# Routed experts: lists in tile order, and the gather of tile t+6 asked for ahead of the scatter-add of tile t

## The chip, the core and the metric

The kernel is one program on one core of a Trainium2 chip. The metric is its time on the device in microseconds (us). One core has five engines that run their own instruction streams and meet in semaphores: PE (TensorE, matmuls; its weight loads are listed as PEld), DVE (VectorE), ACT (ScalarE), POOL (GpSimd) and SP (SyncE, which here only issues transfers). Transfers are carried out by 16 DMA engines. In the profile "q" behind an engine's name is its sequencer.

## What is computed

Sixteen sequences of 56 tokens (896 tokens, width 512) attend to 1500 context rows each; then every token goes through a mixture of 16 experts, of which it takes 4, and through a shared expert.

```python
def _L0_xattn_ref(text, features, Wq, bq, Wk, bk):
    Q = jnp.einsum('btx,dx->btd', text, Wq) + bq
    K = jnp.einsum('bpx,dx->bpd', features, Wk) + bk
    scores = jnp.einsum('btd,bpd->btp', Q, K) * scale
    return jnp.einsum('btp,bpd->btd', jax.nn.softmax(scores, axis=-1), features)

def _L0_ffn_ref(hidden_states, gate_w, bias, Wg, Wu, Wd, Sg, Su, Sd):
    scores = jax.nn.sigmoid(x @ gate_w.T) + bias
    topk_w, topk_idx = jax.lax.top_k(scores, TOPK)
    topk_w = topk_w / (jnp.sum(topk_w, axis=-1, keepdims=True) + 1e-20)
    cw = jnp.sum(jax.nn.one_hot(topk_idx, E, dtype=x.dtype) * topk_w[..., None], axis=1)
    z = jax.nn.silu(jnp.einsum('th,eih->eti', x, Wg)) * jnp.einsum('th,eih->eti', x, Wu)
    out = jnp.einsum('eti,ehi->th', z * cw.T[:, :, None], Wd)
    return out + jax.nn.silu(x @ Sg.T) * (x @ Su.T) @ Sd.T

x = x + _L0_xattn_ref(_layernorm(x), ctx_4096, Wq, bq, Wk, bk)
x = x + _L0_ffn_ref(_layernorm(x), gate_w, bias, Wg, Wu, Wd, Sg, Su, Sd)
```

## The kernel before

**Stages.** Until about 262 us the program does attention, pair of sequences by pair. Then come seven tiles of 128 tokens through the shared expert (tiles 0 to 6), and from about 320 us the routed tiles: tile numbers 7 to 40, 34 tiles in all. A routed tile is up to 128 tokens of one expert; an expert has one or more tiles in a row. Which tokens a tile holds is known only once all tokens are gated, so the kernel builds lists (`list_rows`) and a plan of small tables (`lay_tables`, read into registers by `entry`).

**One routed tile.** POOL gathers the tile's 128 rows from `h_rows` in DRAM into `taken[i]` (`gather`, L444; i is the parity, so there are two buffers). PE transposes it into bank b4 (`taken_transpose`, four matmuls of L500). ACT rounds it to `taken_hi` (L908), DVE makes the rest `taken_lo` (L1299). PE multiplies with the expert's weights into b6 or b7 (`up_hi`, `up_lo`, L680), ACT and DVE make `z_rows`, PE transposes that (L703), ACT and DVE split it again into `zt_hi` (L918) and `zt_lo` (L1315), and PE does the second product (`down`, L680) into one of two banks. ACT copies the result to `y_sb` (`keep_y`, L926, two buffers), and POOL adds it to the output rows in DRAM (`add`, L459, a scatter-add by an indirect DMA).

**The software pipeline.** PE's step goes: transposition of z of tile t-1, `up_lo(t)`, transposition of tile t+1, `down(t-1)`, `up_hi(t+1)`. ACT's step goes: `z_to_hi(t-1)`, `half(t)`, `taken_to_hi(t+1)`, `keep_y(t-2)`, `name_add(t-2)`, `more_thirds(t+1)`. DVE's: `z_to_lo(t-1)`, `silu_rows(t)`, `taken_to_lo(t+1)`, `take_weight(t+1)`, `name_take(t+3)`, `more_thirds(t+1)`. `more_thirds` splits the next expert's weights into a rounded part (ACT, L897, `w_hi`) and the rest (DVE, L1280, `w_lo`), a third of an expert at a time; SP loads them (L383, `w_raw`, three buffers). `keep_y(t)` waits for `added[i]`, that is until the scatter-add of tile t-2 has landed. `down(t)` waits for `keep_y(t-2)`.

**What sets the order on POOL.** The queue is written out by hand: four adds of the shared expert, two gathers, and so on, then a loop of `add(t)`, `gather(t+5)`. `add(t)` waits for the adds of all earlier experts to land (table `T_FIRST`), for its row numbers `add_at` (ACT, `name_add`, L931) and for `y_sb`. `gather(t)` waits for its row numbers `take_at` (DVE, `name_take`, L1306), and DVE writes these only after it has read tile t-2's weights.

## Time and profile before

| | us |
|---|---|
| median of 3 runs | 547.0 (546.81 to 549.09) |
| the profiled execution, its own time | 546.24 |
| its span, from the first to the last instruction | 544.5 |
| PE busy | 481.4 (88%) |
| POOL busy | 119.3 (22%) |
| DVE, ACT busy | 260.0, 155.8 |

The span is the time in which instructions ran; 1.74 us of the execution's own time lie around it. A busy PE is the lower bound that everything else has to hide under. In the views below, a timeline row reads: start in us, length in us, engine, line, operation, what is written <- what is read, and in brackets how long the engine had been idle and what ended that.

### The profile page before, as it was taken

How to read it: one execution, taken by the hardware profiler on the slowest of the kernel's cores; microseconds unless marked ns; L12 is line 12 of the kernel's file. 1: busy time of each engine (PE TensorE's matmuls, PEld its weight loads, DVE VectorE, ACT ScalarE, POOL GpSimd, SP SyncE). 2: the span in 40 equal slices, each digit the busy share in tenths (PEclk: the TensorE clock that was granted, in tenths of full speed). 3: DMA queues.
4: the chain of work that ended last, by engine and by line, in shares of the span. 5: the costliest groups of instructions: out<-in, count | busy, mean ns of one | idle time of the engine just before them, and what ended most of it. 6: DMA issues, size and time to landing. Idle time of an engine off the chain costs nothing.

```text
span 544.5 us, 10804 instructions
## 1 busy us (share of the span) xinstructions
PE 481.4 (88%) x2472; PEld 291.5 (54%) x2473; DVE 260.0 (48%) x707; ACT 155.8 (29%) x303; POOL 119.3 (22%) x100
## 2 busy tenths in 40 slices
PE   4999999999999999998789869779998898899960
PEld 1565354453636363543358636567776666676740
DVE  3223345462737354352537864625565466555420
ACT  0001321020202020210213253435455456444430
POOL 1000000000000000000002233335554465335531
PEclk9989999999999999999899979979999899899985
DMA  9999999999999999999646676785858687445452
GB/s 212 393 419 427 398 424 415 409 427 396 424 402 426 403 422 404 422 426 415 258 127 174 150 202 191 235 254 94 221 100 265 137 207 210 78 88 98 98 64 32
DMA packets 28231, 149.04 MB, mean 274 GB/s; under 512 B 4072, under 2 KB 4200, under 8 KB 16424
## 3 DMA queue, kind: packets, MB, share of 16 engines
q1 hardware_dynamic: 15832, 123.08, 57.1%
q0 software_dynamic: 8720, 20.21, 20.5%
q10 hardware_dynamic: 3664, 5.57, 3.3%
q8 instruction: 7, 0.11, 0.1%
q14 instruction: 8, 0.07, 0.0%
HBM read 133.84 MB, written 15.01 MB: 273 GB/s over the span
## 4 chain that ended last, share of the span: by engine, by line
PE 49%; DMA 33%; issue 7%; DVE 3%; ACT 2%; POOLq 1%; ACTq 1%; POOL 1%; DVEq 1%; SPq 0%
DMA ctx_cols<-in_ctx_t 15%; PE b L680 13%; PE scores L550 11%; PE b L574 8%; DMA taken<-h_rows,take_at 8%; DMA out<-y_sb,add_at 5%; PE b L538 4%; PE b L500 4%; PE scores L512 2%; PE scores L680 2%; PE b L564 1%; DMA w_qk<-in_wk 1%; DMA out<-y_sb,shared_at 1%; DMA h_rows<-h 1%; POOL out L459 1%
## 5 line engine op out<-in xcount | busy, mean ns | idle before, releaser
L550 PE MATMUL scores<-ctx_cols,g_t 128*64 128x500 f32 x384 | 85.2, 586 | 2.6 <-DMA ctx_cols<-in_ctx_t 2.5
L574 PE MATMUL b<-ctx_rows,probs_t 125*64 125x512 f32 (+1 forms) x384 | 86.0, 598 | 0.0
L459 POOL DMA_INDIRECT out<-y_sb,add_at x34 | 54.5, 1604 | 89.0 <-ACT add_at L931 46.8
L423 POOL TENSOR_TENSOR rstd<-var_eps,neg_half 128x1 f32<-128x1 f32 x16 | 8.8, 549 | 268.4 <-DVE var_eps L1022 268.4
L680 PE MATMUL b<-w_hi,taken_hi 128*128 x136 | 56.2, 414 | 1.1 <-ACT taken_hi L908 1.1
L680 PE MATMUL b<-w_lo,taken_hi 128*128 x136 | 54.8, 403 | 0.0
L1280 DVE TENSOR_TENSOR w_lo<-w_raw,w_hi (+1 forms) x33 | 39.7, 1223 | 30.2 <-ACT w_hi L897 26.6
L550 PEld LDWEIGHTS scores<-ctx_cols,g_t 128*64 128x64 f32 x384 | 26.1, 136 | 51.8 <-issue 46.0
L574 PEld LDWEIGHTS b<-ctx_rows,probs_t 125*64 125x64 f32 (+1 forms) x384 | 26.3, 137 | 48.0 <-issue 47.1
L444 POOL DMA_INDIRECT taken<-h_rows,take_at x34 | 42.7, 1257 | 28.4 <-DVE take_at L1306 20.2
L897 ACT CAST w_hi<-w_raw (+1 forms) x33 | 33.8, 1047 | 29.0 <-PE b L680 9.1
L500 PE MATMUL b<-cst,taken 128*128 128x128 f32 x164 | 26.6, 287 | 17.1 <-DMA taken<-h_rows,take_at 15.2
L680 PE MATMUL b<-w_hi,taken_lo 128*128 x136 | 40.0, 416 | 0.0
L1053 DVE TENSOR_REDUCE row_max<-scores 128x1 f32<-128x1500 f32 x8 | 13.8, 1721 | 50.4 <-PE scores L550 50.4
L836 ACT COPY h_t_now<-b 128x512 f32<-128x512 f32 x7 | 4.1, 585 | 110.6 <-PE b L500 110.6
L500 PEld LDWEIGHTS b<-cst,taken 128*128 128x128 f32 x164 | 19.5, 146 | 28.3 <-issue 25.8
L1299 DVE TENSOR_TENSOR taken_lo<-b,taken_hi 128x512 fp32r<-128x512 f32 x41 | 28.1, 685 | 11.6 <-ACT taken_hi L908 11.6
L538 PE MATMUL b<-xn_t,w_fold 128*128 128x128 f32 x256 | 32.0, 286 | 1.4 <-ACT xn_t L820 1.4
L680 PEld LDWEIGHTS b<-w_hi,taken_hi 128*128 128x128 f32 x136 | 26.8, 197 | 11.0 <-issue 4.9
L908 ACT CAST taken_hi<-b 128x512 fp32r<-128x512 f32 x41 | 24.0, 587 | 30.1 <-PE b L500 28.6
L538 PEld LDWEIGHTS b<-xn_t,w_fold 128*128 128x128 f32 x256 | 30.7, 200 | 1.9 <-issue 1.0
L918 ACT CAST zt_hi<-b 128x256 fp32r<-128x256 f32 x41 | 15.2, 371 | 54.4 <-PE b L703 54.1
(213 smaller groups left out, 677.2 us busy)
## 6 DMA issues: line engine op xcount, KB each, us to landing
ctx_rows<-in_ctx SPq DMA_DIRECT2D x48, 1024.0 KB, 19.5
ctx_cols<-in_ctx_t SPq DMA_DIRECT2D x32, 1500.0 KB, 22.8
w_raw<-in_experts SPq DMA_DIRECT2D x11, 1536.0 KB, 7.5
h_rows<-h ACTq DMA_DIRECT2D x16, 115.5 KB
taken<-h_rows SPq DMA_DIRECT2D x7, 264.0 KB, 3.1
out<-xs ACTq DMA_DIRECT2D x2, 784.0 KB
shared_raw<-in_shared SPq DMA_DIRECT2D x1, 1536.0 KB, 32.4
xs<-in_x ACTq DMA_DIRECT2D x12, 112.0 KB
```

The source lines that it names most:

```text
L444: nc.gpsimd.indirect_dma_start(taken[i][:, :], None, h_rows[:, :], bass.IndirectOffsetOnAxis(ap=take_at[i][:, 0:1], axis=0)).then_inc(gath ...
L459: nc.gpsimd.indirect_dma_start(out[:, :], bass.IndirectOffsetOnAxis(ap=add_at[i][:, 0:1], axis=0), y_sb[:, i * DIM:(i + 1) * DIM], None, c ...
L500: last = nc.tensor.transpose(bank[:, k * P:(k + 1) * P], src[:, k * P:(k + 1) * P], ident)
L538: last = nc.tensor.matmul(b7[:, m * P:(m + 1) * P], w_fold[:, k, m * P:(m + 1) * P], xn_t[:, k, :], start=(k == 0), stop=(k == KD - 1))
L550: last = nc.tensor.matmul(scores[HALF * b:HALF * (b + 1), n, 0:CHUNK], g_t[:, k, HALF * b:HALF * (b + 1)], ctx_cols[:, at:at + CHUNK], sta ...
L574: last = nc.tensor.matmul(b3[HALF * b:HALF * (b + 1), :], probs_t[0:rows_in(p), at:at + HALF], ctx_rows[0:rows_in(p), g, b, c * DIM:(c + 1 ...
L680: return nc.tensor.matmul(bank, a[:, k, :], w[:, bass.ds(at + k * n, n)], start=start, stop=stop)
L897: nc.scalar.copy(w_hi[:, bass.ds(at, THIRD)], w_raw[:, bass.ds(at, THIRD)]).then_inc(hi_ready, 1)
L908: nc.scalar.copy(taken_hi[:].rearrange("p k n -> p (k n)"), b4[:, :]).then_inc(taken_hi_ready, 1)
L918: nc.scalar.copy(zt_hi_cols[:], b5[:, 0:INNER]).then_inc(zt_hi_ready, 1)
L1280: nc.vector.tensor_tensor(w_lo[:, bass.ds(at, THIRD)], w_raw[:, bass.ds(at, THIRD)], w_hi[:, bass.ds(at, THIRD)], ALU.subtract).then_inc(l ...
L1299: nc.vector.tensor_tensor(taken_lo[:].rearrange("p k n -> p (k n)"), b4[:, :], taken_hi[:].rearrange("p k n -> p (k n)"), ALU.subtract).th ...
```

## The change

- **Lists in tile order.** The row numbers of all lists (`place_at`) are transposed by PE (`lay_places`), copied by ACT (`keep_places`), and multiplied by a 0/1 matrix `tile_picks` (`pick_tiles`), so that `tile_at` and `tile_to` hold one column per tile. `name_take` and the naming of the add then read a column by the tile number. The tables `T_COL` and `T_EXPERT` and the reads of them into registers are gone; `take_weight` picks the expert's column by a comparison (one DVE instruction on 128x16). Two matmuls are added to `lay_tables`, two small DVE instructions (`keep_picks`) behind the copy of the plan.
- **POOL.** The loop is `gather(t+6)`, then `add(t)`. A gather also waits for `tt_ready`, that is until PE has transposed tile t-2, which freed its buffer. `add_at` is now copied by POOL itself, in `add`, after the own parity's earlier add has landed; `add` then waits for that copy. ACT's `name_add` is gone. In the opening, gathers 7 and 8 stand before `add_shared(3)`, and `gather(12)` stands before the loop.
- **DVE.** `take_weight` and `name_take` stand before `silu_rows` in the step.
- **SP.** The first two weight loads are issued back to back, on two semaphores; the second no longer waits for the first to land.

On POOL, in the loop over routed tiles, one half of the loop body before (out is the kernel's output, y_sb a tile's result, added0 and added1 count landed adds):

```order
L323 TENSOR_LOAD plan
L323 ISA x2
L451 ISA
L453 ISA [waits added0]
L455 REGISTER_ALU [waits added1]
L457 REGISTER_ALU [waits add_named]
L459 DMA out_0<-y_sb,add_at1 1024x512 [waits ysb_ready]
L442 REGISTER_ALU
L444 DMA taken0<-h_rows,take_at0 128x528 [waits take_named]
```

and the same half now:

```order
L463 REGISTER_ALU [waits take_named]
L465 DMA taken1<-h_rows,take_at1 128x528 [waits tt_ready]
L331 ISA
L331 TENSOR_LOAD plan
L331 ISA x2
L472 ISA
L474 ISA [waits added1]
L474 COPY add_at1<-tile_to 128x1
L476 ISA
L478 REGISTER_ALU [waits added0]
L482 DMA out_0<-y_sb,add_at1 1024x512 [waits ysb_ready,add_named]
```

The gather moved ahead of the add and got a wait on PE's transposes; the copy of `add_at` moved from ACT to POOL.

On ACT, from the copy of a result to the next third of weights, before:

```order
L926 COPY y_sb<-b3 128x512 [waits added0]
L323 ISA
L323 TENSOR_LOAD plan
L323 ISA x2
L931 ISA
L931 COPY add_at0<-list_to 128x1
L323 ISA
L323 TENSOR_LOAD plan
L323 ISA x2
L939 COMPARE_AND_BRANCH
L942 ISA [waits yt_ready]
```

and now:

```order
L968 COPY y_sb<-b3 128x512 [waits added0]
L331 ISA
L331 TENSOR_LOAD plan
L331 ISA x2
L981 COMPARE_AND_BRANCH
L984 ISA [waits yt_ready]
```

One table read and the copy of `add_at` left the step; the wait for the landed add stayed in front of the copy of the result.

The diff, cut to its core:

```diff
...
                 sp.dma_start(w_raw[:, bass.ds(at, WFREE)],
-                             experts[bass.ds(e, 1), :, :].rearrange("a p n -> (a p) n")).then_inc(raw_loaded, 16)
-                sp.wait_ge(raw_loaded, (k + 1) * 16)
+                             experts[bass.ds(e, 1), :, :].rearrange("a p n -> (a p) n")
+                             ).then_inc(raw_first if isinstance(k, int) and k == 0 else raw_loaded, 16)
+
+            def raw_there(k):
+                sp.wait_ge(raw_loaded, k * 16)
                 sp.sem_inc(raw_ready, THIRDS)
...
             load_raw(1)
+            sp.wait_ge(raw_first, 16)
+            sp.sem_inc(raw_ready, THIRDS)
+            raw_there(1)
             sp.wait_ge(yt_ready, SHARED)
             load_raw(2)
+            raw_there(2)
             n_turns = sp.value_load(plan[0:1, T_TURNS:T_TURNS + 1], min_val=TOPK, max_val=EXPERTS)
                 load_raw(k)
+                raw_there(k)
...
+                pool.wait_ge(added[t % 2], t // 2 * 16 + 16)
                 pool.wait_ge(ysb_ready, t + 1)
...
                 settle(pool)
+                pool.wait_ge(tt_ready, t - 1)
+                settle(pool)
                 nc.gpsimd.indirect_dma_start(
...
                 first = entry(pool, T_FIRST, t - SHARED, TILES + SHARED)
-                pool.wait_ge(added[0], pool.snap((first + 1) // 2 * 16 + 16, min_val=16, max_val=16 * TILES))
+                pool.wait_ge(added[i], t // 2 * 16 + 16)
                 settle(pool)
-                pool.wait_ge(added[1], pool.snap(first // 2 * 16 + 16, min_val=16, max_val=16 * TILES))
-                settle(pool)
-                pool.wait_ge(add_named, t - (SHARED - 2))
+                nc.gpsimd.tensor_copy(add_at[i][:], tile_to[:, bass.ds(t - SHARED, 1)]).then_inc(add_named, 1)
+                others = first // 2 if i == 0 else (first + 1) // 2
+                pool.wait_ge(added[1 - i], pool.snap(others * 16 + 16, min_val=16, max_val=16 * TILES))
                 settle(pool)
                 pool.wait_ge(ysb_ready, t + 1)
+                settle(pool)
+                pool.wait_ge(add_named, t + 1)
                 settle(pool)
...
             add_shared(2)
-            add_shared(3)
             pool.wait_ge(init_stored, 16)
             pool.wait_ge(h_stored, PAIRS * 32 + 16)
-            pool.wait_ge(plan_ready, 1)
-            n_inner = inner_pairs(pool)
             gather(SHARED, 1)
             gather(SHARED + 1, 0)
+            add_shared(3)
             add_shared(4)
             add_shared(6)
+            gather(SHARED + 5, 0)
+            pool.wait_ge(tiles_named, 1)
+            pool.wait_ge(plan_ready, 1)
+            n_inner = inner_pairs(pool)
             with pool.Fori(0, n_inner - 1) as pair:
                     t = pair * 2 + (SHARED + k)
+                    gather(t + 6, 1 - k)
                     add(t, 1 - k)
-                    gather(t + 5, k)
             t = n_inner * 2 + (SHARED - 2)
-            add(t, 1)
-            gather(t + 5, 0)
-            for k in range(1, 6):
+            for k in range(6):
                 add(t + k, 1 - k % 2)
...
                 last.then_inc(table_rows_ready, 1)
+                for at, column in ((C_PICK, place_col), (C_EXPERT, expert_t)):
+                    last = nc.tensor.matmul(scores[:, 0, at:at + AHEAD], column[:].to_broadcast([P, P]),
+                                            ident[:, 0:AHEAD], start=True, stop=True)
+                last.then_inc(picks_ready, 1)
+
+            def lay_places():
+
+                pe.wait_ge(plan_ready, 1)
+                pe.wait_ge(places_ready, 1)
+                nc.tensor.transpose(scores[:, 2, 0:P], place_at[:], ident).then_inc(places_laid, 1)
+
+            def pick_tiles():
+
+                pe.wait_ge(places_kept, 1)
+                nc.tensor.matmul(scores[:, 2, P:P + AHEAD], place_t[:], tile_picks[:], start=True, stop=True
+                                 ).then_inc(tiles_picked, 1)
...
             shared_transpose(6)
+            lay_places()
             down(4, 0, shared_hi, shared_lo, 0)
+            pick_tiles()
             up_hi(6, 0, shared_hi, shared_lo, 0)
...
             taken_to_hi(6)
+            keep_places()
             keep_y(3, 1)
...
                 keep_y(t - 2, i)
-                if not isinstance(t, int):
-                    name_add(t - 2, i)
                 more_thirds(t + 1)
-            act.wait_ge(list_named, 1)
             more_thirds(SHARED)
...
                 ch.link(nc.vector.scalar_tensor_tensor(raw_at[:], lists[:, :, 0], float(P), lists[:, :, 1], ALU.mult, ALU.add))
-                ch.mark(nc.vector.tensor_tensor(list_at[:, 0:LISTS], raw_at[:], fill[:], ALU.add))
-                ch.link(nc.vector.tensor_tensor(place_at[:], raw_at[:], fill[:], ALU.add))
-                ch.link(nc.vector.tensor_scalar(wrapped[:], place_at[:], float(PAIR_TOKENS), float(TOKENS), ALU.is_lt, ALU.mult))
-                ch.link(nc.vector.scalar_tensor_tensor(wrapped[:], empty[:], float(PAIR_TOKENS), wrapped[:], ALU.mult, ALU.add))
-                ch.mark(nc.vector.scalar_tensor_tensor(list_to[:, 0:LISTS], place_at[:], -float(PAIR_TOKENS), wrapped[:], ALU.add,
-                                                       ALU.add))
-                dve.wait_ge(dve_step, ch.now())
-                dve.sem_inc(list_named, 1)
-
+                nc.vector.tensor_tensor(place_at[:, 0:LISTS], raw_at[:], fill[:], ALU.add).then_inc(places_ready, 1)
+
+            def tile_rows():
+
+                dve.wait_ge(tiles_picked, 1)
+                places = scores[:, 2, P:P + AHEAD]
+                ch.link(nc.vector.tensor_copy(tile_at[:], places))
+                name_take(SHARED, 1)
+                name_take(SHARED + 1, 0)
+                ch.mark(nc.vector.tensor_scalar(wrapped[:], places, float(PAIR_TOKENS), float(TOKENS), ALU.is_lt, ALU.mult))
+                ch.link(nc.vector.tensor_scalar(empty_at[:], places, float(TOKENS), float(PAIR_TOKENS), ALU.is_ge, ALU.mult))
+                ch.link(nc.vector.tensor_tensor(wrapped[:], wrapped[:], empty_at[:], ALU.add))
+                nc.vector.scalar_tensor_tensor(tile_to[:], places, -float(PAIR_TOKENS), wrapped[:], ALU.add, ALU.add
+                                               ).then_inc(tiles_named, 1)
+
+            def keep_picks():
+
+                dve.wait_ge(picks_ready, 1)
+                nc.vector.tensor_scalar(tile_picks[:], scores[:, 0, C_PICK:C_PICK + AHEAD], upto[:], None, ALU.is_equal)
+                ch.mark(nc.vector.tensor_copy(expert_row[:], scores[:, 0, C_EXPERT:C_EXPERT + AHEAD]))
...
-
-                col = entry(dve, T_COL, t - SHARED, LISTS + EXPERTS - 1)
-                nc.vector.tensor_copy(take_at[i][:], list_at[:, bass.ds(col, 1)]).then_inc(take_named, 1)
+                nc.vector.tensor_copy(take_at[i][:], tile_at[:, bass.ds(t - SHARED, 1)]).then_inc(take_named, 1)
             def take_weight(t, i):
-                e = entry(dve, T_EXPERT, t - SHARED, EXPERTS - 1)
-                nc.vector.tensor_copy(taken_w[:, i:i + 1], taken[i][:, bass.ds(e + DIM, 1)]).then_inc(w_ready, 1)
+                dve.wait_ge(gathered[i], (t - SHARED) // 2 * 16 + 16)
+                settle(dve)
+                dve.wait_ge(z_rows_ready, t - 1)
+                settle(dve)
+                nc.vector.scalar_tensor_tensor(picked_w[:, i * EXPERTS:(i + 1) * EXPERTS], iota16, expert_row[:, bass.ds(t - SHARED, 1)],
+                                               taken[i][:, DIM:ROW], ALU.is_equal, ALU.mult, accum_out=taken_w[:, i:i + 1]
+                                               ).then_inc(w_ready, 1)
...
             nc.vector.tensor_copy(plan[:], scores[0:1, 2, 0:TABLES * TILES]).then_inc(plan_ready, 1)
+            keep_picks()
             shared_silu(4)
             list_rows()
-            dve.wait_ge(plan_ready, 1)
-            name_take(SHARED, 1)
             shared_silu(5)
             taken_to_lo(6)
-            name_take(SHARED + 1, 0)
+            tile_rows()
             dve.wait_ge(hi_ready, 1)
...
             n_inner = inner_pairs(dve)
-            taken_to_lo(SHARED)
             take_weight(SHARED, 1)
             name_take(SHARED + 2, 1)
+            taken_to_lo(SHARED)
                 z_to_lo(t - 1)
+                take_weight(t + 1, 1 - i)
+                name_take(t + 3, 1 - i)
                 silu_rows(t, i)
                 taken_to_lo(t + 1)
-                take_weight(t + 1, 1 - i)
-                name_take(t + 3, 1 - i)
                 more_thirds(t + 1)
...
```

## Rows read from the trace of the kernel before

**Rows 1.** The profile's page: granted PE clock in 40 equal slices, tenths of full speed.

```profile
PEclk9989999999999999999899979979999899899985
```

**Rows 2.** The waits of PE: who waited <- for whom: us in total, times, longest.

```profile
PE b L500 <- DMA taken<-h_rows,take_at: 15.2, 9, 5.2
```

**Rows 3.** Timeline of PE: the first and the longest wait for a gather.

```profile
320.98 1.09 PE L500 MATMUL b<-cst,taken 128*128 128x128 f32 x4 [3.07 <-DMA taken<-h_rows,take_at]
...
356.62 1.09 PE L500 MATMUL b<-cst,taken 128*128 128x128 f32 x4 [5.21 <-DMA taken<-h_rows,take_at]
```

**Rows 4.** The chain that ended last: start us, us, what (14 matmuls, three times).

```profile
357.71 4.64 PE b L680 x14
...
379.56 3.36 PE b L680 x14
...
426.71 4.31 PE b L680 x14
```

**Rows 5.** Timeline of POOL around the longest gather wait.

```profile
345.87 2.30 POOL L459 DMA_INDIRECT out<-y_sb,add_at  x1 [5.33 <-issue]
348.47 1.01 POOL L444 DMA_INDIRECT taken<-h_rows,take_at  x1 [0.30 <-issue]
```

**Rows 6.** Timeline of all engines, one step without a stall (tile 16 to 17).

```profile
378.96 0.60 PE L500 MATMUL b<-cst,taken 128*128 128x128 f32 x4
...
380.16 0.59 ACT L926 COPY y_sb<-scores 128x512 f32<-128x512 f32 x1
...
380.95 0.19 ACT L931 COPY add_at<-list_to 128x1 int32 x1 [0.20 <-issue]
...
382.09 1.05 ACT L897 CAST w_hi<-w_raw  x1 [0.95 <-issue]
...
384.16 0.63 PE L500 MATMUL b<-cst,taken 128*128 128x128 f32 x4
...
384.74 0.42 DVE L1315 TENSOR_TENSOR zt_lo<-b,zt_hi 128x256 fp32r<-128x256 f32 x1
...
385.82 0.63 PE L680 MATMUL scores<-w_hi,zt_lo 128*128 x2
```

**Rows 7.** Timeline of POOL: start latency, gaps, and the add of tile 13.

```profile
2.01 1.33 POOL L418 DMA_DIRECT2D out<-zero_rows  x2 [0.69 <-POOL zero_rows L412]
...
382.13 1.57 POOL L459 DMA_INDIRECT out<-y_sb,add_at  x1 [1.63 <-ACT add_at L931]
...
493.67 1.57 POOL L459 DMA_INDIRECT out<-y_sb,add_at  x1 [0.39 <-issue]
```

**Rows 8.** Groups of POOL by line: count, then busy us and mean ns.

```profile
L444 POOL DMA_INDIRECT taken<-h_rows,take_at x34 | 42.7, 1257 | 28.4 <-DVE take_at L1306 20.2 <-issue 8.2
```

**Rows 9.** The page's groups: the splitting of weights, a third of an expert each.

```profile
L897 ACT CAST w_hi<-w_raw (+1 forms) x33 | 33.8, 1047 | 29.0 <-PE b L680 9.1
```

**Rows 10.** Timeline of POOL and of DVE: a gather's issue beside a w_lo.

```profile
368.28 1.88 POOL L444 DMA_INDIRECT taken<-h_rows,take_at  x1 [0.30 <-issue]
...
368.05 1.23 DVE L1280 TENSOR_TENSOR w_lo<-w_raw,w_hi  x1 [1.27 <-ACT w_hi L897]
```

**Rows 11.** Adds (L459), issue to landing: all 34, then tile 8's and tile 26's.

```profile
DMA to landing us min/median/max: 4.5/4.9/8.8
...
DMA to landing us min/median/max: 7.1/7.1/7.1
...
DMA to landing us min/median/max: 6.7/6.7/6.7
```

**Rows 12.** The waits of ACT from 300 us on.

```profile
ACT y_sb L926 <- DMA out<-y_sb,add_at: 5.4, 2, 4.6
```

**Rows 13.** Timeline of DVE and POOL: naming and issue of the first gather.

```profile
313.13 0.16 DVE L1306 COPY take_at<-list_at 128x1 int32 x1 [1.16 <-issue]
...
314.18 1.02 POOL L444 DMA_INDIRECT taken<-h_rows,take_at  x1 [0.97 <-DVE take_at L1306]
```

More of the change, by code:

```diff
@@ L36 @@
 TILES = 48
-TABLES = 8
+TABLES = 6
 SHARED = TOKENS // P
-T_TURNS, T_COL, T_EXPERT, T_PIECES, T_TURN, T_FIRST, T_LOAD, T_HALF = (i * TILES for i in range(TABLES))
+AHEAD = TILES + 4
+T_TURNS, T_PIECES, T_TURN, T_FIRST, T_LOAD, T_HALF = (i * TILES for i in range(TABLES))
 C_ID, C_TRI, C_IOTA, C_REGION = 0, P, 2 * P, 2 * P + EXPERTS
@@ L104, in before @@
                 left -= n
-            assert left >= 0
-            if left:
+            if left > 0:
                 sb(f"{name}_rest", [P, left])
@@ L1154, in _ @@
             nc.vector.tensor_copy(shared_at[:], shared_place[:]).then_inc(shared_named, 1)
-            for rows in (list_at, list_to):
-                ch.mark(nc.vector.tensor_scalar(rows[:, LISTS:], dump_row[:].to_broadcast([P, EXPERTS]), -float(P), None,
-                                                ALU.add))
+            ch.mark(nc.vector.tensor_scalar(place_at[:, LISTS:], dump_row[:].to_broadcast([P, EXPERTS]), -float(P), None,
+                                            ALU.add))
             wide = [P, PAIRS, TILES_MAX]
```

48 lines of the change are left out of this document (27 added, 21 removed).

## Prediction, made before the changed kernel ran

> **What bounds the kernel now.** I read the granted clock, then the waits of PE, then the chain and a single step in the timeline. The attention stage is untouched by the change, so only the time from about 310 us on counts. There PE works through 34 routed tiles, and what it waits for is mostly the gather of a tile's rows: 15.2 us in nine waits [rows 2]. The first of them (3.07 us) is the start of the routed stage, the longest (5.21 us) belongs to tile 12 [rows 3]. The gather of tile 12 was not slow to be named: it stood on POOL behind the first scatter-add, and that one waited 5.33 us for all the shared expert's adds to land [rows 5]. The reader should see that POOL's order, not its load, made that gap. After the gap PE is also slow: the same 14 matmuls take 4.64 us and, after a later gap, 4.31, against 3.36 in a stretch without one [rows 4]; slices 26 and 31 of the granted clock, counted from 0, are 7 and 8 tenths [rows 1], so part of those slices ran at the lower of the two levels, 1.2 GHz.
>
> **A step without a stall.** I call T the end of a tile's four transposes: 379.56 us for tile 16, 384.79 for tile 17, a step of 5.23 [rows 6]. ACT starts to copy the result of tile t-3 at T + 0.60 (380.16), then names the add, splits a third of weights (382.09), DVE makes its other part and then `zt_lo`, which ends at 385.16, and PE reads it at 385.82 [rows 6]. So in a step with one third the copy may start 0.66 us later before PE stalls. It waits for a landed add, and in the whole routed stage it did so visibly only twice, 5.4 us in all [rows 12].
>
> **What the change removes.** (1) The waits for gathers. A gather now needs only T of the tile two ahead of it, which is 2 × 5.23 = 10.5 us before its rows are used. Issue and landing together took at most 8.0 of that in the trace (the longest wait's gather, issued at 348.47 for 356.62) [rows 3, 5]. All but the first wait go: 15.2 − 3.07 = 12.1 us. (2) The slow clock behind the two longer gaps: (4.64 − 3.36) + (4.31 − 3.36) = 2.2 us, and about 0.5 us each for the transposes before them (1.09 against 0.60) [rows 3, 4, 6], 3.2 in all. (3) On ACT the naming of the add, 0.20 + 0.19 us [rows 6]; it makes the 0.66 us of spare into 1.05. On DVE two table reads per step; DVE waits for ACT there, so I count nothing. Gain: 15.3 us.
>
> **What it leaves as it is.** The first gather. `take_at` was written at 313.13 and the gather began at 314.18 [rows 13]. The name now comes by two more matmuls and a copy on ACT behind `list_rows`, but without 1.16 us of reading a register [rows 13] and without three list operations. I put the two equal and keep −1 to +1.5 us for the range. The second weight load starts some 7 us earlier, but PE then waits for the first gather; I count nothing, and the two loads contend with that gather as the second one did before. The wait of PE for `tiles_named` lies long behind.
>
> **What it adds.** `add(t)` now stands behind `gather(t+6)`, and that gather waits for the transposes of tile t+4. Before, the add of tile 13 began at 382.13, 2.66 us before T of tile 17 [rows 6, 7]. Now it begins after T. The sum from T: POOL's start after a semaphore, 0.9 (0.99 after ACT, from 381.14 to 382.13; 0.89 after DVE, from 313.29 to 314.18) [rows 6, 7, 13]; the gather's issue, 1.26 on the mean [rows 8]; then the copy of `add_at` and the wait for it. That copy does not stand in this trace. Its lower bound is the plain gap between two issues, 0.39, as if the copy were hidden; the nearest rows above are POOL's wait for its own result, 0.69, on top of that gap [rows 7], so 1.1 is my value, and with a wait as after DVE and a slow copy 1.8 the upper bound. The add lands 4.9 us after its issue [rows 11], and ACT may start 0.1 later. Together 0.9 + 1.26 + 1.1 + 4.9 + 0.1 = **8.3 us after T(t)**, for the copy of tile t-2, which ACT wants at T(t+1) + 0.60 and may start until 5.23 + 0.60 + 1.05 = **6.9 us after T(t)**. It is late by 1.4 us in a step with one third, and without a third it is not late.
>
> Seven of the 34 adds (tiles 8, 9, 14, 18, 19, 23 and 26, from 7.1 to 6.7 us, the longest 8.8) took about 7.4 us, all of them beside a weight load [rows 11]. Then the copy is late by 8.3 + 2.5 − 6.9 = 3.9 us.
>
> A stall of PE also puts off the two deadlines behind it, so of two or three late steps in a row about one pays. There are 33 thirds [rows 9], six of them ahead of the loop; from tile 11 on sixteen steps have one. I take four of the seven slow adds to pay 3.9 us (15.6), and of the twelve other steps six to pay 1.4 (8.4): 24.0. Some of these stalls are as long as the gaps that now bring the slow clock: +2. **Sum:** 24.0 + 2 − 15.3 = +10.7. On the execution's own 546.24 us that is 556.9; its median of 547.0 is 0.76 higher, so 557.7, and I say 557.5.
>
> **The bounds of the unknown.** With the copy hidden (0.39) and a gather's issue of 1.0 the lateness is 0.4 and 2.9 us: 4 × 2.9 + 6 × 0.4 = 14.0, +1 − 15.3 = −0.3, about 546.7. With 1.8 and an issue of 1.88 as beside DVE's `w_lo` [rows 10] it is 2.8 and 5.3: 4 × 5.3 + 6 × 2.8 = 38.0, +3 − 15.3, about 572.7.
>
> The Trainium skill (DMA: Bandwidth & Descriptors, "Anatomy of one DMA") gives a transfer from GpSimd about 2.0 us plus its bytes at 436 GB/s, which would be 2.6 us for the 256 KB of an add. By that the copy would never be late and the time would be about 532. The rows show 4.5 to 8.8 us, so the trace does not agree, and I go by the rows.
>
> **Rivals.** *A, the ring holds (faster).* The copy waits for nothing that PE feels. For it: ACT's waits show two only, and each term has a lower end. The point at which it decides is the start of the add: up to T + 1.9 us (6.9 − 4.9 − 0.1) nothing is lost in a quiet step; and the adds, which now begin some 6 us later against the weight loads, could mostly miss them. Then two slow adds at most cost 1.2 each: 547.0 − 15.3 + 2.4 = 534. Against it: even the smallest terms make T + 2.3. 0.22.
> *B, an even trade.* The lower ends above, 546.7: 0.12.
> *C, POOL's issue is held up as well (slower still).* A gather beside DVE's `w_lo` took 1.88 us [rows 10]. The later copy moves `w_lo` to just after T, which is where the gather is now issued. Then each paying step costs 0.6 more: 24.0 + 10 × 0.6 + 3 − 15.3 = +17.7, about 565. 0.18. Beside this stands the Trainium skill (GPSIMD Engine Reference, "Key points"): GpSimd shares its SBUF interfaces with VectorE, and instructions with two SBUF inputs contend. The trace agrees, 1.88 against a mean of 1.26 us.
> *D, the change does not start gathers earlier,* because the new wait on PE takes the add's place. It cannot hold them long: T of two tiles ahead is 10.5 us before the use. It is in the range, not a case of its own.
>
> **The numbers.** Forecast 557.5, chance 0.48. Its own range is 550 to 564. Of a median of 547 about 2.7 us (0.5%) can be told from no change. Slower holds the forecast and C, 0.66; the same holds B, 0.12; faster holds A, 0.22. The range leaves out the lower part of A and the upper tail of C: 540 to 568.
>
> **What the changed profile would show.** If right: PE has hardly a wait for a gather behind the first; ACT's copy to `y_sb` waits for a landed add in a dozen steps or more; PE waits for `zt_hi` or `zt_lo` instead; adds begin about 3.3 us after T; the clock's sevens move to other places. If the adds begin less than 2 us after T, or ACT's waits for them stay near 5 us, the forecast is wrong and A holds. If PE still waits for gathers, D does. If the first gather starts beyond 315.5 us, the opening has its own loss, which I left out.

## The result: slower by 3.9%, and the profile after

The changed kernel took 566.99 us (median of 4 runs, 564.73 to 572.24), the kernel of before 546.90 (4 runs, 543.52 to 549.09). The ratio is 1.0387, 95% interval [1.029, 1.0483]: 20 us more, where 10.5 were forecast. The sign and one of the two mechanisms were forecast. The outer range (540 to 568) held the time, the forecast's own (550 to 564) did not, and the loss was about twice the one of the sum. The profiled execution after took 572.24 us, its span 570.1.

The page of the kernel after, busy time of PE and the granted clock in 40 slices, which answers [rows 1]:

```profile
PE 494.3 (87%) x2475; PEld 299.6 (53%) x2476; DVE 259.3 (45%) x742; ACT 149.0 (26%) x269; POOL 121.2 (21%) x134
...
PEclk9969999999999999997999798899898987899995
```

From slice 22 on (counted from 0, the routed tiles) eight slices of the clock lie below 9 tenths, the last slice left aside, where five did before. PE was busy for 12.9 us longer than before (481.4) with practically the same matmuls: part of the loss is a slow clock. The profiled execution is the slowest of its four, 5.2 us above their median, and has the lowest granted clock of them (0.944 against 0.950 to 0.963), so its trace shows somewhat more of this than the median does.

The waits of the kernel after from 300 us on (engine, line, waited for: us in total, times, longest), which answer [rows 2] and [rows 12]:

```profile
ACT y_sb L968 <- DMA out<-y_sb,add_at: 82.4, 27, 7.0
POOL taken L465 <- issue: 76.6, 25, 10.4
DVE w_lo L1326 <- ACT w_hi L939: 73.3, 21, 8.3
...
PE b L719 <- ACT zt_hi L960: 25.7, 11, 7.7
POOL out L482 <- ACT y_sb L968: 17.8, 11, 4.0
POOL taken L465 <- DVE take_at L1350: 14.9, 3, 6.4
```

and those of PE alone:

```profile
PE scores L719 <- ACT zt_hi L960: 8.6, 5, 3.6
PE b L523 <- DMA taken<-h_rows,take_at: 3.2, 2, 2.4
```

PE's wait for gathers went from 15.2 us to 3.2, as forecast. In its place PE waits 34.3 us for ACT's `zt_hi` (3.9 before), and ACT is late because its copy to `y_sb` waited for a landed scatter-add 27 times, 82.4 us in all, against twice and 5.4 us before. A wait was taken away from PE and a longer one put on the engine that feeds it.

To divide the loss I cut the same stretch out of four kernels, from the end of the transposes of tile 7 to the end of those of tile 40. Columns: us from:to, length, busy PE, PEld, DVE, ACT, POOL (count), granted clock, DMA share, GB/s. Kernel before:

```profile
322.07:517.93 195.86, 176.29 (x787) 132.06 (x788) 105.01 (x226) 94.77 (x192) 91.96 (x64) 0.95 0.66 160
```

Kernel after:

```profile
321.92:543.95 222.03, 185.15 (x786) 136.11 (x786) 103.79 (x255) 88.22 (x161) 90.03 (x95) 0.92 0.59 141
```

The stretch grew by 26.2 us, 8.9 of it in busy time of PE for 786 matmul rows in place of 787 (the clock, 0.92 against 0.95) and 17.3 in idle time (36.9 against 19.6). This is the profiled execution, whose own time is 26.0 us above the one of before; of the medians' 20 us each part is correspondingly less. The opening did not change: PE ended tile 7's transposes at 321.92 against 322.07.

### The profile page after: what moved, and what is told of

Its sections match the earlier page's. It is cut to its first block, busy times and chain, and to the rows that moved or that the text cites. A ratio compares the mean times of both kernels' runs of the same rounds, so it can differ in the third digit from the quotient of the medians.

```text
span 570.1 us, 10514 instructions
## 1 busy us (share of the span) xinstructions
PE 494.3 (87%) x2475; PEld 299.6 (53%) x2476; DVE 259.3 (45%) x742; ACT 149.0 (26%) x269; POOL 121.2 (21%) x134
## 4 chain that ended last, share of the span: by engine, by line
PE 53%; DMA 19%; issue 12%; DVE 4%; ACT 4%; ACTq 2%; POOLq 2%; DVEq 1%; POOL 1%; SPq 0%
DMA out<-y_sb,add_at 15%; PE b L597 15%; PE scores L573 14%; PE b L719 6%; PE b L561 6%; PE scores L535 2%; PE b L523 2%; PE b L587 2%; ACT w_hi L939 2%; DMA w_raw<-in_experts 2%; DMA w_qk<-in_wk 1%; ACTq L331 1%; DMA taken<-h_rows,take_at 1%; PE b L610 1%; POOLq L331 1%
## 5 line engine op out<-in xcount | busy, mean ns | idle before, releaser
L482 POOL DMA_INDIRECT out<-y_sb,add_at x34 | 56.3, 1656 | 38.4 <-ACT y_sb L968 17.8
L719 PE MATMUL b<-w_hi,taken_hi 128*128 x136 | 58.7, 432 | 1.2 <-ACT taken_hi L950 1.1
L719 PE MATMUL b<-w_lo,taken_hi 128*128 x136 | 56.9, 419 | 0.0
L465 POOL DMA_INDIRECT taken<-h_rows,take_at x34 | 33.4, 982 | 103.6 <-issue 76.6
L719 PE MATMUL b<-w_hi,zt_hi 128*128 x34 | 16.7, 491 | 26.7 <-ACT zt_hi L960 25.7
L1364 DVE TENSOR_TENSOR zt_lo<-b,zt_hi 128x256 fp32r<-128x256 f32 x41 | 17.3, 421 | 39.5 <-ACT zt_hi L960 39.3
L719 PEld LDWEIGHTS b<-w_hi,taken_hi 128*128 128x128 f32 x136 | 28.2, 207 | 12.8 <-issue 6.0
L561 PE MATMUL b<-xn_t,w_fold 128*128 128x128 f32 x256 | 33.2, 292 | 1.4 <-ACT xn_t L862 1.4
L719 PEld LDWEIGHTS b<-w_lo,taken_hi 128*128 128x128 f32 x136 | 28.1, 206 | 6.4
L523 PE MATMUL b<-cst,taken 128*128 128x128 f32 x164 | 25.1, 275 | 3.8 <-DMA taken<-h_rows,take_at 3.2
```

The lines of the kernel that those rows point to most:

```text
L465: nc.gpsimd.indirect_dma_start(taken[i][:, :], None, h_rows[:, :], bass.IndirectOffsetOnAxis(ap=take_at[i][:, 0:1], axis=0)).then_inc(gath ...
L482: nc.gpsimd.indirect_dma_start(out[:, :], bass.IndirectOffsetOnAxis(ap=add_at[i][:, 0:1], axis=0), y_sb[:, i * DIM:(i + 1) * DIM], None, c ...
L523: last = nc.tensor.transpose(bank[:, k * P:(k + 1) * P], src[:, k * P:(k + 1) * P], ident)
L561: last = nc.tensor.matmul(b7[:, m * P:(m + 1) * P], w_fold[:, k, m * P:(m + 1) * P], xn_t[:, k, :], start=(k == 0), stop=(k == KD - 1))
L719: return nc.tensor.matmul(bank, a[:, k, :], w[:, bass.ds(at + k * n, n)], start=start, stop=stop)
L1364: nc.vector.tensor_tensor(zt_lo_cols[:], b5[:, 0:INNER], zt_hi_cols[:], ALU.subtract).then_inc(zt_lo_ready, 1)
```

## Where the forecast missed: one turn of a loop in the trace

As in the prediction, T is the end of a tile's four transposes. Every piece that the sum named is there in the trace. Timeline of the kernel after, POOL, the gather of tile 20 and the add of tile 14 (start, length, what; in brackets the idle time before and what ended it):

```profile
394.88 0.98 POOL L465 DMA_INDIRECT taken<-h_rows,take_at  x1 [1.29 <-issue]
396.05 0.18 POOL L474 COPY add_at<-tile_to 128x1 int32 x1 [0.20 <-issue]
397.23 1.61 POOL L482 DMA_INDIRECT out<-y_sb,add_at  x1 [1.00 <-POOL add_at L474]
```

The copy and the wait for it take 1.4 us here and 1.06 where nothing else comes between, as in the rows from 405.60 on below (I had 1.1). But the next gather and add, of tiles 21 and 15, stand far from the transposes of tile 19 (T = 399.55), and the rows of the other engines tell why. Kernel after, one stretch, POOL, ACT, DVE and PE:

```profile
391.98 1.61 POOL L482 DMA_INDIRECT out<-y_sb,add_at  x1 [0.86 <-issue]
...
405.60 0.98 POOL L465 DMA_INDIRECT taken<-h_rows,take_at  x1 [6.75 <-issue]
406.57 0.20 POOL L474 COPY add_at<-tile_to 128x1 int32 x1
407.63 1.61 POOL L482 DMA_INDIRECT out<-y_sb,add_at  x1 [0.86 <-issue]
...
400.18 0.58 ACT L968 COPY y_sb<-scores 128x512 f32<-128x512 f32 x1 [6.16 <-DMA out<-y_sb,add_at]
401.32 1.04 ACT L939 CAST w_hi<-w_raw  x1 [0.55 <-issue]
402.27 0.36 ACT L960 CAST zt_hi<-b 128x256 fp32r<-128x256 f32 x1
...
402.70 1.23 DVE L1326 TENSOR_TENSOR w_lo<-w_raw,w_hi  x1 [7.07 <-ACT w_hi L939]
403.84 0.42 DVE L1364 TENSOR_TENSOR zt_lo<-b,zt_hi 128x256 fp32r<-128x256 f32 x1
...
404.32 0.15 DVE L1350 COPY take_at<-tile_at 128x1 int32 x1
...
403.17 0.50 PE L719 MATMUL scores<-w_hi,zt_hi 128*128 x1 [3.62 <-ACT zt_hi L960]
403.51 0.59 PE L719 MATMUL scores<-w_lo,zt_hi 128*128 x1
403.90 0.63 PE L719 MATMUL scores<-w_hi,zt_hi 128*128 x1
```

Follow it round. The add of 391.98 lands only at 400.08 (8.1 us, next fence). So the `y_sb` copy starts at 400.18, `w_hi` at 401.32, `w_lo` at 402.70, `zt_lo` at 403.84, and only behind that, on DVE, is `take_at` written, at 404.32. The gather that needs this name starts at 405.60, 6.05 us after the transposes that freed its buffer, and the add behind it at 407.63, whose landing ACT's copy of two tiles later needs in turn. The add's lateness comes back to its own start: a closed loop of one turn in two steps. The bracket behind the gather says "issue" although the name had held it; the timeline of the two engines side by side shows it, the bracket doesn't.

The chain that ended last has the same loop in order of time (start, length, what), kernel after:

```profile
374.22 4.93 DMA out<-y_sb,add_at
...
379.37 5.04 DMA out<-y_sb,add_at
...
385.66 1.06 ACT w_hi L939
...
391.98 8.10 DMA out<-y_sb,add_at
...
401.32 1.05 ACT w_hi L939
...
407.63 4.23 DMA out<-y_sb,add_at
```

Of the 40 us from 370 on, 55.7% of this chain are the landings of adds; the matmuls carry next to nothing of it. At 379.37 the chain also holds an add that started 0.2 us after the landing of the add before it: a tile that opens a new expert waits for the adds of the one before, as in the kernel of before. That wait is not what makes adds late: 21 of the 28 adds of tiles 7 to 34 start 2.0 to 2.4 us after the start of the gather in front of them, which is issue, copy and wait. An add is late because its gather is. Read in this way, 24 of the 28 gathers of tiles 13 to 40 have their name as the last thing to come and start 1.0 to 1.4 us after it, 16 of them 2.3 us or more behind their transposes; for the other four the transposes came last, by less than 0.2 us. Of the 30 adds of tiles 7 to 36, ten start 3.1 to 3.9 us behind T of the tile four ahead (I had 3.3), eighteen 4.4 to 12.4 us. The prediction put all of them at T + 3.3, since it took the name as written long before.

The worst turn shows a second thing that the sum left out. It took one third of weights in each of sixteen steps, but in three more (behind T of tiles 21, 29 and 30 in the trace of before) three thirds are split. Kernel after, ACT, DVE and POOL:

```profile
478.51 0.58 ACT L968 COPY y_sb<-b 128x512 f32<-128x512 f32 x1 [6.98 <-DMA out<-y_sb,add_at]
479.65 2.94 ACT L939 CAST w_hi<-w_raw  x3 [0.56 <-issue]
...
481.04 3.50 DVE L1326 TENSOR_TENSOR w_lo<-w_raw,w_hi  x3 [8.34 <-ACT w_hi L939]
...
486.10 0.98 POOL L465 DMA_INDIRECT taken<-h_rows,take_at  x1 [10.37 <-issue]
```

A late landing (the add of 468.37, 10.04 us) and three thirds in a row put the gather of tile 32 10.41 us behind its transposes, and PE's longest gap, 7.70 us up to 483.39, lies here.

So theory 1: the loss is the forecast's open chain (gather behind the transposes, add behind the gather, landing) plus a closed loop through the name. The rival, theory 2: the names are late only because everything is, and the open chain with its slow landings is the whole loss.

## Experiments

All times are medians; ratios are against the kernel of before, measured together with the run, with a 95% interval. Us worked out from ratios are of 547. The diffs are cut to the lines that matter ("...").

### 1. A gather one tile less deep

```diff
...
-            gather(SHARED + 5, 0)
...
-                    gather(t + 6, 1 - k)
+                    gather(t + 5, k)
                     add(t, 1 - k)
             t = n_inner * 2 + (SHARED - 2)
+            gather(t + 5, 0)
```

> The changed kernel with the gather one tile less deep: GpSimd asks for gather(t+5) and then scatter-adds tile t; all else as changed. Gather(t+5) waits for the transposes of tile t+3, which in the changed kernel's trace start 5.2 to 8 us before those of tile t+4. Theory 1 (the time went because the add stands behind a gather that waits for the transposes of t+4): the add starts 2 to 3 us before the transposes of t+4 again, as in the trace of before, the waits of ACT's y_sb copy for the add's landing fall from 82 us to under 20, the gathers stay early, and the time is 531 to 537 us. Rival (the cost is the order itself, any gather ahead of the add, by its 0.98 us of issue and the copy of add_at behind it): the add is later than before by 2 us in each of 33 steps, 2 x 10 steps of them uncovered, and the time is 545 to 555 us.

Measured: 532.70 us, ratio 0.9768 [0.9717, 0.982], the best of the study together with the two variants of it below. ACT's waits in this kernel and the page's clock:

```profile
ACT y_sb L968 <- DMA out<-y_sb,add_at: 17.5, 8, 4.9
```

```profile
PEclk9969999999999999999899999899999999999995
```

and the stretch from tile 7 to tile 40:

```profile
320.87:505.29 184.42, 172.60 (x788) 128.62 (x788) 104.78 (x263) 89.22 (x161) 95.82 (x96) 0.99 0.69 171
```

One tile of depth decides between +3.9% and −2.3%. The gather of t+5 waits for the transposes of t+3, so the add starts before T of t+4 in 23 of 30 cases (mostly 0.3 to 2.1 us before it; the latest of all 3.9 us behind it), the `y_sb` waits fall from 82.4 to 17.5 us, and the rival of the order itself (545 to 555) falls. Against before, idle time of PE fell by 7.7 us (19.57 to 11.82) and its busy time by 3.7.

### 2. The order of before, all else changed

```diff
...
-                    gather(t + 6, 1 - k)
                     add(t, 1 - k)
+                    gather(t + 5, k)
...
```

> The changed kernel with GpSimd's order of before: add(t), then gather(t+5); the lists in tile order, the names in front of silu_rows, the copy of add_at on GpSimd and the early weight loads stay. If the POOL order is what costs, this is at or below the time before, 541 to 547 us, with gathers that still come 3 to 4 us after the transposes that free them and PE waits for them of 8 to 15 us. If the new naming (the copy of add_at on GpSimd, 1.06 us ahead of the add, and the weight picked by a 16-wide product on DVE) costs by itself, it is above 549 us.

Measured: 540.80 us, 0.9879 [0.9835, 0.9923], just under the lower end of what I wrote. PE's waits for gathers stand almost as before:

```profile
PE b L524 <- DMA taken<-h_rows,take_at: 14.1, 10, 3.1
```

So the loss of the change lies in POOL's queue (order and depth of the gather) alone; the rest of the change is worth 1.2%. Two more runs look for what in the rest that is.

> The kernel of e2_add_first (add, then gather(t+5)) with the weight pick and the name behind taken_to_lo(t+1), their place in the kernel of before. What is left of the change is the lists in tile order, the copy of add_at on POOL in place of ACT's, the pick by a product, the fewer register reads and the opening. e2 took 1.2% off the time of before. If the earlier name gave that, this is level with before; if the registers and ACT's name_add gave it, it stays 0.8 to 1.2% below.

The kernel of experiment 2 with `take_weight` and `name_take` moved back behind `taken_to_lo`: 540.16 us, 0.991 [0.9872, 0.9948]. The earlier name gives nothing while the add stands first. What is left are the lists in tile order with fewer register reads, ACT without `name_add`, and the opening. Which of the first two gave it was not tested.

> The kernel of before with only the change on SP: the first two weight loads are asked for back to back. I counted nothing for it: the first wait of PE in the routed stage is for the first gather, which starts at 314.2 us whatever the loads do. Expected within 2 us of before. If the two loads contend with the first gather more than one did, its landing moves from 321 to 322 us or later and the time rises by 1 to 2 us; if the earlier second load frees ACT, it falls by as much.

Of the opening the two weight loads together, in the kernel of before: 544.82 us, 0.9964 [0.9924, 1.0004]. Nothing to tell from before, as counted.

### 3. The exchange on POOL in the kernel of before

```diff
-                    add(t, 1 - k)
                     gather(t + 5, k)
+                    add(t, 1 - k)
```

> The kernel of before with one exchange on GpSimd: gather(t+5) and then add(t), nothing else. The gather loses its place behind the add's wait for y_sb, so it starts 2 to 3 us earlier, and PE's waits for gathers (15 us in the trace of before) and the slow clock behind them (3 us) go: 529 to 536 us. The add gets 1 us of gather issue ahead of it, which it has to give: it starts 2.3 to 3.3 us ahead of the transposes of t+4 now. If the rival holds, that an add behind any gather is late for ACT's y_sb copy, the time is 545 us or more.

Measured: 550.31 us, 1.0092 [1.0057, 1.0127]. A clear miss: the same exchange that made experiment 1 made this kernel slower. In its trace (an execution of 556.09 us, 1% above that median) POOL waits for names:

```profile
POOL taken L444 <- DVE take_at L1306: 73.6, 27, 8.2
```

A gather that stands in front of an add passes on whatever it waits for. Here the name comes at the end of DVE's step, and the add has to wait for it too. To see how much of it is the place of the name, I gave the kernel of experiment 1 that place:

```diff
                 z_to_lo(t - 1)
-                take_weight(t + 1, 1 - i)
-                name_take(t + 3, 1 - i)
                 silu_rows(t, i)
                 taken_to_lo(t + 1)
+                take_weight(t + 1, 1 - i)
+                name_take(t + 3, 1 - i)
```

> The kernel of e1_gather5_first with the weight pick and the name put behind taken_to_lo(t+1) on DVE, their place in the kernel of before. This tells apart the two reasons why e9 (before, with its two POOL instructions exchanged) took 550 and e1 took 533. If the place of the name on DVE is the reason, gathers start 4 to 7 us after the transposes again, POOL's wait for take_at is over 60 us, adds start behind the transposes of t+4, and the time is 545 to 552 us. If the table reads from registers and ACT's name_add, which e9 keeps and e1 has not, are the reason, it stays at 532 to 536 us.

Measured: 538.84 us, 0.9854 [0.9774, 0.9933]. Between my two numbers: of the 17.6 us between experiments 3 and 1 the place of the name is some 5 (0.0086 in the ratios), and even that is not firm, since the two intervals just overlap. Gathers start 2.8 to 8.5 us after T in place of 0.9 to 5.8. The larger part must lie with what the old kernel does besides, the register reads ahead of each name and `name_add` on ACT, in front of which adds waited too; I did not take these apart.

### 4. The name in front of z_to_lo

```diff
+                take_weight(t + 1, 1 - i)
+                name_take(t + 3, 1 - i)
                 z_to_lo(t - 1)
-                take_weight(t + 1, 1 - i)
-                name_take(t + 3, 1 - i)
```

> The changed kernel with one move on DVE: the weight pick of tile t+1 and the naming of tile t+3 stand in front of z_to_lo(t-1) and not behind it. Theory 1a (a closed loop over two steps: late y_sb copy, late zt_hi copy, late z_to_lo, late name, late gather, late add, late y_sb copy): gathers start within 1.5 us of the transposes that free them in nearly every step instead of half of them, the y_sb waits fall by a third, and the time falls by 6 to 12 us, to 555 to 561 us. Rival 1b (the names are late only because everything is; what holds the add is the transposes of t+4 plus a landing of 5 to 8 us): gather starts move with the transposes, and the time stays within 2 us of 567.

Measured: 562.98 us, 1.0322 [1.0259, 1.0385]. That is 4 us below the change, between the two forecasts, and the intervals overlap, so that it is a gain at all is not shown. The trace tells why it could only be small: `w_lo` of the step before still stands in front of the name, and 15 of the 28 gathers start 1.0 to 1.1 us after it. The loop was not opened. The same move in the kernel of experiment 1:

> The kernel of e1_gather5_first with the weight pick of tile t+1 and the name of tile t+3 put in front of z_to_lo(t-1) on DVE. In e1's trace seven gathers still start 3.2 to 5.8 us after the transposes that free them, and the adds behind them are level with or behind the transposes of t+4. If their names are what they wait for, these gathers start within 2 us, the last stalls for zt_hi shrink, and the time is 529 to 532 us. If they wait for the add in front of them (which itself waits for the one two tiles back to land), nothing moves: 532 to 534 us.

534.87 us, 0.9787 [0.9729, 0.9844]: no difference, since there the loop has slack.

### 5. The name taken out of the loop

Now the name stands in front of `w_lo` too, one step ahead of its place in the change:

```diff
...
                 z_to_lo(t - 1)
-                take_weight(t + 1, 1 - i)
-                name_take(t + 3, 1 - i)
                 silu_rows(t, i)
                 taken_to_lo(t + 1)
+                if more:
+                    take_weight(t + 2, i)
+                    name_take(t + 4, i)
                 more_thirds(t + 1)
...
```

> The changed kernel with the weight pick and the name moved one step ahead on DVE: in step t, behind taken_to_lo(t+1) and in front of w_lo, the weight of tile t+2 is picked and tile t+4 is named. In the changed kernel's trace 23 of 28 gathers start 1.0 to 1.4 us after their name, and the name stands behind zt_lo and w_lo, which wait for ACT's w_hi behind the late y_sb copy; e3 took the name from behind zt_lo only, and 15 gathers stayed bound by it. Here no name waits for w_lo or zt_lo. Loop theory: nearly all gathers start 0.9 us after the transposes that free them, adds 3.3 us after them, and what is left is the sum of my prediction, 553 to 560 us with the slow clock. Rival (the open chain alone, gather behind the transposes of t+4 and then the add's landing, is the whole loss and the names only follow it): 562 us or more, as e3.

Measured: 551.35 us, 1.012 [1.007, 1.017], a little under the range that I wrote. This is the deciding run: POOL's order is that of the change, the same amount of work is done, and 14.6 us are gone (2.67%, from the ratios; the medians differ by 15.6). POOL's waits in this kernel:

```profile
POOL taken L465 <- PE b L523: 63.8, 26, 6.7
ACT y_sb L968 <- DMA out<-y_sb,add_at: 60.0, 22, 6.3
```

and its timeline at the gather of tile 22 (T of tile 20 is 403.21):

```profile
404.06 0.98 POOL L465 DMA_INDIRECT taken<-h_rows,take_at  x1 [4.26 <-PE b L523]
405.05 0.23 POOL L474 COPY add_at<-tile_to 128x1 int32 x1
406.12 1.61 POOL L482 DMA_INDIRECT out<-y_sb,add_at  x1 [0.85 <-issue]
```

No gather is bound by its name; 27 of 28 start 0.84 to 0.93 us after their transposes, and 22 of the 30 adds start at T + 2.9 to T + 4.0, nine of them at 2.9 to 3.0: 0.86 + 0.98 + 1.06. This comes nearest to the kernel that the prediction had summed up, and it is +6.6 us (1.2%) against a forecast of +10.7. The stretch from tile 7 to 40:

```profile
319.62:523.11 203.49, 177.71 (x787) 129.92 (x787) 103.81 (x263) 89.09 (x161) 96.89 (x96) 0.97 0.65 155
```

Against before: +6.2 us of idle time, +1.4 of busy time. Theory 2 falls.

> The same earlier names in the kernel of e1_gather5_first. There nine gathers of 28 are bound by their name and fifteen by the add in front of them on POOL. If the names still cost, 528 to 531 us; if PE's matmuls and the add's landings set the end by now, 532 to 534 us, as e1 and e5.

The same names in the kernel of experiment 1: 532.92 us, 0.9773 [0.9728, 0.9818], level with it. Once the gathers and adds are early enough, more earliness buys nothing. This also rules out that experiment 5 gained by a shorter step of DVE itself: the same move is worth nothing here, nor was the move the other way in the kernel of experiment 2. And the two kernels of this experiment, measured together, differ in the depth of the gather alone: with its name out of the loop the gather one tile deeper costs 551.35 − 532.92 = 18.4 us. That, not the +6.6, is the price of the open chain; the +6.6 is what is left of it after the gain.

### 6. Light weight loads

Which part of the loss hangs on adds that land slowly beside a weight load? The loads from the fourth on are cut to an eighth of their bytes (seven eighths of those weights are left out), in the kernels of after, of before and of experiment 5:

```diff
-                sp.dma_start(w_raw[:, bass.ds(at, WFREE)],
-                             experts[bass.ds(e, 1), :, :].rearrange("a p n -> (a p) n")
+                width = WFREE if isinstance(k, int) else WFREE // 8
+                sp.dma_start(w_raw[:, bass.ds(at, width)],
+                             experts[bass.ds(e, 1), :, 0:width].rearrange("a p n -> (a p) n")
...
```

> The changed kernel, its weight loads from the fourth on cut to an eighth of their bytes; the rest of the weights is left from earlier loads, so part of the computation's data is left out, and all instructions but those loads keep their size. It shows how much of the loss hangs on landings beside a weight load (8.1 us against 4.2 to 5). The loss is 20 us. If the slow landings carry it, as my sum had it (15.6 of 24.0), adds land in 4.5 to 5.3 us throughout, waits of the y_sb copy fall from 82 to under 40 us, and the time is 545 to 553 us. If the loop over name, gather and add carries it, it is 555 us or more.

> The kernel of before with the same cut of its weight loads to an eighth (the same part of the data is left out): what light loads give to a kernel whose adds are early. Its waits for gathers come from the add in front of each gather and from POOL's place, so 2 to 6 us less than before at most: 540 to 544 us. If it falls as far as the changed kernel does, the light loads tell nothing of the adds.

> The kernel of e14 (names in front of w_lo, so that no gather waits for its name) with the weight loads from the fourth on cut to an eighth of their bytes, as in e4: that part of the weights is left out. Light loads took 17 us off the changed kernel and 8 us off the one of before. By my sum the open chain costs nothing in a step without a slow landing except 1.4 us in six steps: then this is 534 to 541 us, about level with the light kernel of before (538.8 us), since the gathers' waits are gone too. If the open chain is late by itself whatever the landing takes, adds at the transposes + 3 us keep ACT's y_sb copy waiting and PE behind it, and it is 545 us or more.

Measured, as ratio to before with full loads:

| | full loads | light loads |
|---|---|---|
| before | 1 | 0.9867 [0.9792, 0.9943], 538.79 us |
| names out of the loop (experiment 5) | 1.012 [1.007, 1.017] | 0.9931 [0.9893, 0.9969], 540.26 us |
| the change | 1.0387 [1.029, 1.0483] | 1.008 [1.0032, 1.0128], 550.24 us |

The changed kernel's time is where I put it for slow landings as the cause (545 to 553), but its waits at `y_sb` did not fall under 40 us with it (73.9, below); the kernel of before came out just under my 540 to 544. With light loads the chain of the changed kernel shows landings between 4.1 and 5.4 us each (one row of 9.59 us holds two in a row); with full loads the same chain has 6.76, 8.10, 7.38, 6.04 and 10.04 beside others of 4.2 to 5.0. Read down the columns, 1% being 5.5 us: with full loads the open chain, net of what the earlier gathers gain, leaves 1.2% (6.6 us) and the loop costs 2.7% (14.6 us); with light loads 0.6% (3.5) and 1.5% (8.2). The intervals are about 1% wide, so these are rough shares: slow landings make somewhat under half of either, and the loop costs some 8 us even without them. With light loads the `y_sb` copy of the changed kernel still waits often:

```profile
ACT y_sb L969 <- DMA out<-y_sb,add_at: 73.9, 29, 4.9
```

and with the name out of the loop it does so too, but PE feels half of it (its waits for `zt_hi` come to 10.9 us against 20.0):

```profile
ACT y_sb L969 <- DMA out<-y_sb,add_at: 50.6, 26, 5.0
```

A third `y_sb` buffer would test the deadline itself; it was not tried.

## Why the prediction was right and wrong, point by point

- **Gathers' waits go, 12.1 us: right as a wait, too much as a gain.** 15.2 to 3.2 us [rows 2], with 2.4 of it at the first gather, which was left out of the gain. Experiment 1 has 3.7 us less of busy time (I had 3.2 for the slow clock) and 7.7 less of idle time; the rest of the 12.1 came back as other waits. In time it gains 12.7 us (2.3%) where I had 15.3, and only 8.1 of that is POOL's queue (540.80 − 532.70). The other 1.2% experiment 2 has too: register reads, `name_add` and the opening, for which I counted nothing. That two errors nearly cancel here is luck.
- **The opening, nothing: right as far as the profiles show.** First gather at 314.98 against 314.18, PE at tile 7 0.15 us earlier.
- **The open chain, T + 8.3 us: right in its parts.** POOL's start 0.86 (I had 0.9), issue 0.98 (1.26), copy and wait 1.06 (1.1), landing, in the rows of its chain, 4.2 to 5.0 or 6 to 10 (4.9 or 7.4). With the loop opened its price is 18 to 19 us (18.4 in experiment 5) against the 26.0 of the sum (24.0 and 2 for the clock), so this term was too large. Of the bounds, the upper one is worked out 1 us too high: 0.9 + 1.88 + 1.8 + 4.9 + 0.1 is 2.7 us late, which makes 571.7.
- **The step that failed: "Before, the add of tile 13 began ... Now it begins after T. The sum from T: POOL's start after a semaphore, 0.9".** It measures every gather from its transposes and takes the name as written. The name stands on DVE behind `zt_lo`, and that behind `w_lo`, `w_hi` and the very `y_sb` copy that the add makes late. The prediction wrote that DVE "waits for ACT there, so I count nothing": the right observation, with the wrong conclusion. Four of the 28 gathers were bound by their transposes, 24 by the name. This is 14.6 us. In the terms of the sum, all from the ratios: −12.7 for the gain (I had −15.3), +19.3 for the open chain (I had +26.0), +14.6 for the loop (I had nothing), together +21.2, which is 3.87% of 547. The sum came out at +10.7 by one term left out and two that were too large.
- **"from tile 11 on sixteen steps have one": true, and three more have three.** Those three steps are not in the sum, and the largest stall lies in one of them (the fence above from 478.51 on). What they cost by themselves no run separates.
- **"of two or three late steps in a row about one pays": wrong for the same reason as the failed step.** A stall puts off the two deadlines behind it only if it does not put off the add as well. In a loop it does, and the lateness is carried on: the slow landing of 391.98 still shows in the add of 407.63.
- **The slow clock, +2: a term mis-sized.** The balance with the gain was −1.2 us; measured are +8.9 us of busy time, in the slowest of the four executions. In that stretch the kernel after has 18 gaps of PE over 0.3 us where before had 13, up to 7.70 us long, and behind the long ones matmuls of 0.39 us take 0.63, as in the fence above from 403.51 on. In experiment 5 the same term is +1.4, so most of it comes with the loop.
- **Rival A (the ring holds, 534): wrong for this change.** But its point of decision, the add's start at T + 1.9, fits from both sides: with most adds at T − 2 to T + 1.6 (experiment 1, one add later, at T + 3.9) the result is 532.7, with most at T + 2.9 to T + 4.0 it is 551.
- **Rival C (the issue held up by w_lo, 565): near in time, wrong in kind.** This answers [rows 8] in the groups of POOL in the kernel after (busy us, mean ns):

```profile
L465 POOL DMA_INDIRECT taken<-h_rows,take_at x34 | 33.4, 982 | 103.6 <-issue 76.6 <-DVE take_at L1350 14.9 <-PE b L523 12.1
```

  No gather's issue was stretched, because in the loop each gather waits for a name that stands behind `w_lo`, so the two can't meet. In experiment 5, where they can, eight of 34 do and take 1.24 to 1.94 us; the longest (POOL, then DVE):

```profile
433.51 1.94 POOL L465 DMA_INDIRECT taken<-h_rows,take_at  x1 [1.09 <-PE b L523]
...
433.37 1.23 DVE L1326 TENSOR_TENSOR w_lo<-w_raw,w_hi  x1 [3.65 <-ACT w_hi L939]
```

  So what the Trainium skill says of the shared SBUF interfaces of GpSimd and VectorE (GPSIMD Engine Reference, "Key points") agrees with the trace, but the time of C was reached by another road.
- **Rival D, no gather earlier:** false, PE's waits for them are gone.

## What to carry to other kernels

When a queue gets a new instruction in front of one that others wait for, list all that the new one waits for, and follow each back until it ends at something that the change does not delay. If one of them leads back to the delayed instruction, the loss does not stay one step's lateness but is paid on every turn, and with a slow clock on top. Ask ahead only as far as the transfer needs: here one tile less of depth turned +3.9% into −2.3%.

## What the runs showed of the hardware

- A gather's issue on POOL takes 0.98 us: 34 of 34 in the kernel after lie between 952 and 1043 ns, where the mean before was 1.26 [rows 8]. DVE was not idle meanwhile; in 32 of them it made `taken_lo`, which reads the PSUM bank `b4` and one SBUF tile, and the issue did not lengthen. What lengthens it is `w_lo`, which reads two SBUF tiles: 13 issues of the kernel before (1.23 to 1.93 us) and eight of experiment 5 (1.24 to 1.94) all had it beside them. One case goes against this: the gather of tile 8 in the kernel after had a `w_lo` beside it for 0.89 us and took 0.98.
- An instruction of POOL that waits for POOL's own result starts 0.85 us after it even in the best case here (register instructions of the sequencer lie in between), four times the length of the copy itself (0.20 us): a copy of 128 numbers put in front of a transfer costs 1.06 us.
- Weight loads at an eighth of their bytes made the kernel of before 1.3% faster and the changed one 3.1%, which fits adds without slack in the changed kernel.
